# Patch embeddings of tiles 4 to 10 as three fp16 products instead of fp32, and one new wait on VectorE

## The reference, cut to what matters

```
out = jnp.einsum('bnp,dp->bnd', patches, W) + b            # patch embedding
h = jnp.concatenate([cls_tok broadcast, out], axis=1)      # 32 x 37 x 256
h = h + attn(layernorm(h), Wq, Wk, Wv, Wo, bo, betas, mem, z)
h = h + ffn(layernorm(h), shared_w1, shared_w2, experts_w1, experts_w2, gate_w)
```

## Time and profile before

| what | us |
|---|---|
| median of 3 runs | 326.65 (326.32 to 326.92) |
| profiled execution | 325.89 |
| its span in the trace | 324.0 |
| PE busy | 306.7 (95%) |
| DVE busy | 223.4 (69%) |
| ACT busy | 184.5 (57%) |
| POOL busy | 152.1 (47%) |

### The profile page before, as it was taken

The page is one execution under the profiler, slowest core; times in us unless marked ns, Lnnn a source line. Parts: engine busy times, 40 slices in busy tenths (PEclk is TensorE's granted clock), DMA queues, the critical chain, the costliest instruction groups (busy, mean ns, idle before and its releaser), DMA issues.

```text
span 324.0 us, 9888 instructions
## 1 busy us (share of the span) xinstructions
PE 306.7 (95%) x3521; PEld 259.6 (80%) x3521; DVE 223.4 (69%) x502; ACT 184.5 (57%) x355; POOL 152.1 (47%) x208
## 2 busy tenths in 40 slices
PE   8789999999998999999999999999999999999990
PEld 6678788988777999999997777777787787777870
DVE  0637888888898989999886868755554546565530
ACT  1366768878896978476768878733232332323220
POOL 0577747777586322112622344656353544434131
PEclk9999999999999999999999999999999999999998
DMA  7775335322241117814798774243323242333121
GB/s 231 260 222 210 108 111 179 111 83 77 77 124 58 32 31 205 269 24 95 195 275 309 185 239 110 45 67 41 60 42 59 34 67 35 54 48 46 22 34 16
DMA packets 18642, 36.37 MB, mean 112 GB/s; under 512 B 3331, under 2 KB 10982, under 8 KB 18598
## 3 DMA queue, kind: packets, MB, share of 16 engines
q1 hardware_dynamic: 12166, 27.71, 26.2%
q0 software_dynamic: 6432, 8.03, 16.3%
HBM read 28.52 MB, written 7.21 MB: 110 GB/s over the span
## 4 chain that ended last, share of the span: by engine, by line
PE 76%; DVE 9%; DMA 4%; POOL 3%; issue 3%; ACT 2%; SPq 1%; POOLq 1%; DVEq 0%; ACTq 0%
PE bank L820 21%; PE bank L833 14%; PE bank L643 7%; PE bank L835 6%; PE bank L500 6%; PE bank L602 6%; DMA out_rows<-y,add_id 2%; PE bank L525 2%; PE bank L551 2%; DMA weights<-in_patches 2%; PE bank L591 2%; PE bank L565 1%; PE bank L555 1%; DVE weights L1309 1%; PE bank L453 1%
## 5 line engine op out<-in xcount | busy, mean ns | idle before, releaser
L820 PEld LDWEIGHTS bank<-x_t,weights 128*128 x1248 | 87.5, 98 | 25.5 <-issue 0.2
L820 PE MATMUL bank<-x_t,weights 128*128 128x128 f16 x1248 | 103.8, 219 | 0.0
L1002 ACT ACTIVATE act_out<-bank 128x512 f32<-128x512 f32 (+2 forms) x72 | 42.0, 585 | 86.1 <-PE bank L820 71.8
L1270 POOL DMA_INDIRECT out_rows<-y,add_id x26 | 43.0, 1653 | 69.6 <-DVE y L1626 48.1
L833 PE MATMUL bank<-weights,hid_hi 128*128 x192 | 73.3, 382 | 0.2
L1417 DVE SCALAR_TENSOR_TENSOR hid_lo<-act_out,hid_hi 128x512 f16<-128x512 f32 (+2 forms) x72 | 48.6, 680 | 12.5 <-ACT hid_hi L1013 11.0
L835 PE MATMUL bank<-weights,hid_lo 128*128 x192 | 52.3, 273 | 0.0
L1423 DVE SCALAR_TENSOR_TENSOR weights<-stage,weights 128x1024 f16<-128x1024 f32 x36 | 43.0, 1221 | 0.7 <-ACT weights L959 0.7
L959 ACT ACTIVATE weights<-stage 128x1024 f16<-128x1024 f32 x36 | 36.8, 1049 | 0.0
L1237 POOL DMA_INDIRECT slot_rows<-x_rows,gather_id x26 | 28.0, 1075 | 13.0 <-DMA out_rows<-y 5.2
L500 PE MATMUL bank<-weights 128*111 128x256 f32 x132 | 31.3, 386 | 1.6 <-DMA weights<-in_patches 1.1
(11 more groups left out here) (164 smaller groups left out, 522.8 us busy)
## 6 DMA issues: line engine op xcount, KB each, us to landing
stage<-in_w_ffn SPq DMA_DIRECT2D x36, 512.0 KB
weights<-in_patches SPq DMA_DIRECT2D x11, 333.0 KB, 3.3
x_rows<-rows SPq DMA_DIRECT2D x11, 111.0 KB
out_rows<-weights SPq DMA_DIRECT2D x10, 111.0 KB
out_rows<-y POOLq DMA_DIRECT2D x9, 119.0 KB, 5.3
weights<-in_w_embed SPq DMA_DIRECT2D x3, 256.0 KB, 4.2
stage<-in_w_qk SPq DMA_DIRECT2D x1, 512.0 KB, 6.9
slot_rows<-x_rows,gather_id POOLq DMA_INDIRECT x26, 4.1
```

What stands on the lines that cost most here:

```text
L820: mm = nc.tensor.matmul(o, weights[:, bass.ds(base + 2 * k * CHUNK + 2 * (col - col % D) + w * D + col % D, P)], x_t[:, b, (2 * x + k) * P ...
L1002: nc.scalar.activation(d_, s_, ACT.Silu, scale=1.0 / (X_SCALE * W_SCALE)).then_inc(hid_acted, 1)
L1270: nc.gpsimd.indirect_dma_start(out=out, out_offset=bass.IndirectOffsetOnAxis(ap=add_id[:, j:j + 1], axis=0), in_=y[:, y_place(j)], in_offs ...
```

## The change

The weights of the embedding are split once into scaled fp16 high parts (ScalarE, ahead of its first other work) and low parts (VectorE, in step 1). From tile 4 on the patches of a tile are split too: ScalarE makes the high part at the end of step `t-4`, VectorE the low part in step `t-3` (those of tiles 4 and 5 at other places of steps 1 and 2). `embed(t)` is then 18 fp16 matmuls instead of 6 fp32 ones, and `embed_h` undoes the scale while it adds the bias. Tiles 0 to 3 stay fp32. The buffers of the pairs lie in memory that is used only later. The load of a patch buffer now waits for the low part of its last tenant from tile 4 on. From step 5 to step 10 VectorE waits for GpSimd's deviations of the step before, ahead of the weight chunk's low part, behind which the patches' low part now stands.

```diff
+F16_FROM = 4
+P_SCALE = 16.0
+EMBED_PRODUCTS = ((1, 0), (0, 1), (0, 0))
...
             def load_patches(t):
-                if t >= PATCH_RING:
-                    sp.wait_ge(embed_ready, t - PATCH_RING + 1)
+                held = t - PATCH_RING
+                if held >= F16_FROM:
+                    sp.wait_ge(patch_lo, held - F16_FROM + 1)
+                elif held >= 0:
+                    sp.wait_ge(embed_ready, held + 1)
...
             def embed(t):
-                pe.wait_ge(patches_in[t % PATCH_RING], 16 * (t // PATCH_RING + 1))
+                if t < F16_FROM:
+                    pe.wait_ge(patches_in[t % PATCH_RING], 16 * (t // PATCH_RING + 1))
+                else:
+                    pe.wait_ge(patch_lo, t - F16_FROM + 1)
+                if t == F16_FROM:
+                    pe.wait_ge(we_lo, 2)
...
+                if t >= F16_FROM:
+                    for n, (x, w) in enumerate(EMBED_PRODUCTS):
+                        for k in range(PC):
+                            we = we_front[:, k, w] if k < 4 else we_back[:, k - 4, w]
+                            mm = nc.tensor.matmul(embed_bank(t), patch_pair[t % 2][:, x, k * T:(k + 1) * T], we,
+                                                  start=(n == 0 and k == 0), stop=(n == 2 and k == PC - 1))
+                    mm.then_inc(embed_ready, 1)
+                    return
...
+            def split_patches_hi(t):
+                act.wait_ge(patches_in[t % PATCH_RING], 16 * (t // PATCH_RING + 1))
+                if t >= F16_FROM + 2:
+                    act.wait_ge(embed_ready, t - 1)
+                nc.scalar.mul(patch_pair[t % 2][:, 0], s_patch[:, t % PATCH_RING].rearrange("p a b -> p (a b)"),
+                              P_SCALE).then_inc(patch_hi, 1)
+
+            for part_ in range(EMBED_PARTS):
+                act.wait_ge(embed_in[part_], 16)
+                if part_ == 1:
+                    nc.scalar.mul(we_front[:, :, 0], s_we[:, 0:4], W_SCALE).then_inc(we_hi, 1)
+                if part_ == 2:
+                    nc.scalar.mul(we_back[:, :, 0], s_we[:, 4:], W_SCALE).then_inc(we_hi, 1)
...
+                if s in (1, 2):
+                    split_patches_hi(s + 3)
+                if 2 <= s < NT - 4:
+                    split_patches_hi(s + 4)
...
+            def split_patches_lo(t):
+                dve.wait_ge(patch_hi, t - F16_FROM + 1)
+                nc.vector.scalar_tensor_tensor(
+                    out=patch_pair[t % 2][:, 1], in0=s_patch[:, t % PATCH_RING].rearrange("p a b -> p (a b)"),
+                    scalar=P_SCALE, in1=patch_pair[t % 2][:, 0], op0=ALU.mult,
+                    op1=ALU.subtract).then_inc(patch_lo, 1)
...
+                if s == 1:
+                    we_lo_of(0, we_front, s_we[:, 0:4])
+                    we_lo_of(1, we_back, s_we[:, 4:])
...
+                if 5 <= s < NT:
+                    dve.wait_ge(rstd2, s - 4)
                 for c in chunks_at(s):
                     split_lo(c)
+                if 3 <= s < NT - 3:
+                    split_patches_lo(s + 3)
                 if s + 2 < NT:
                     embed_h(s + 2)
+                if s == 1:
+                    split_patches_lo(4)
...
+                    split_patches_lo(5)
```

More of the change, by code:

```diff
@@ L101, in build @@
         y = sb("y", [P, 3, D])
+        we_front = hid_hi.rearrange("p a b -> p (a b)").rearrange("p (k w d) -> p k w d", w=2, d=D)
+        we_back = hid_lo.rearrange("p a b -> p (a b)")[:, 0:2 * 2 * D].rearrange(
+            "p (k w d) -> p k w d", w=2, d=D)
+        patch_pair = [ap[:, 0:2 * PC * T].rearrange("p (w n) -> p w n", w=2) for ap in (
+            act_out.rearrange("p a b -> p (a b)").bitcast(F16),
+            slot_rows.rearrange("p a b -> p (a b)"))]
         space = weights[:, EARLY * EW:].bitcast(F32)
@@ L208, in build @@
         embed_ready = sem("embed_ready")
+        we_hi = sem("we_hi")
+        we_lo = sem("we_lo")
+        patch_hi = sem("patch_hi")
+        patch_lo = sem("patch_lo")
         h_ready = sem("h_ready")
@@ L1300, in embed_h @@
                     dve.wait_ge(rstd1, t - 1)
-                nc.vector.tensor_tensor(h[0:T, t % RING], embed_bank(t), s_eb[0:T],
-                                        ALU.add).then_inc(h_ready, 1)
+                if t < F16_FROM:
+                    nc.vector.tensor_tensor(h[0:T, t % RING], embed_bank(t), s_eb[0:T],
+                                            ALU.add).then_inc(h_ready, 1)
+                else:
+                    nc.vector.scalar_tensor_tensor(out=h[0:T, t % RING], in0=embed_bank(t),
+                                                   scalar=1.0 / (P_SCALE * W_SCALE), in1=s_eb[0:T],
+                                                   op0=ALU.mult, op1=ALU.add).then_inc(h_ready, 1)
                 dve.wait_ge(h_ready, t + 1)
@@ L1361, in proj_lo_of, with we_lo_of @@
                                                op0=ALU.mult, op1=ALU.subtract).then_inc(proj_lo, 1)
+            def we_lo_of(n, dst, src):
+                dve.wait_ge(we_hi, n + 1)
+                nc.vector.scalar_tensor_tensor(out=dst[:, :, 1], in0=src, scalar=W_SCALE, in1=dst[:, :, 0],
+                                               op0=ALU.mult, op1=ALU.subtract).then_inc(we_lo, 1)
+            def split_patches_lo(t):
[4 more added lines that the diff above has]
+                    op1=ALU.subtract).then_inc(patch_lo, 1)
             def xln_lo(t):
```

## The result

| | before | after |
|---|---|---|
| median of 5 runs, us | 326.65 (326.11 to 326.92) | 329.15 (328.54 to 329.70) |
| profiled execution / its span | 325.89 / 324.0 | 329.15 / 327.2 |
| end of step 4 | 45.93 | 46.56 |
| steps 5, 6, 7, 8 | 8.50, 8.96, 8.70, 8.87 | 9.80, 9.32, 9.46, 8.39 |
| end of step 8 | 80.96 | 83.53 |

The changed kernel is slower: ratio 1.0080, with an interval of 1.0067 to 1.0092. The forecast was 327.7; it had the sign, and less than half of the size (+1.05 against +2.5 on the medians). A step is counted as in the prediction, from the end of one `residual`'s statistics to the next. After step 10 the two kernels take the same time. The page's busy times: TensorE has 1.4 us less than before and VectorE 10 more.

The account below looks back on a forecast made before the run. It took TensorE as bound, with the GpSimd loop and VectorE close behind. Steps 1 to 4 +0.1, 5 to 7 +1.44, 8 -0.47: +1.07 on 325.89 gives 326.96, as median 327.7 us; own range 326.9 to 328.5, wide 323.8 to 329.6.

Parts of the forecast that it names:

- the wide range: Whole kernel: 323.8 to 329.6 us, leaving out TensorE's full gain and the sum of both slower rivals.
- the opened lock: Rival, steps 5 to 7: GpSimd's bias add runs between VectorE's two low parts; 9.7 us a step, 329.2 in all; chance 0.13.
- steps 5 to 7: Forecast at 9.2 us each, 27.6 against 26.16 before: +1.44 us.
- step 8: Shorter embedding and the wait, no patches' low part: `embed_h` at 4.75, end at 8.4 against 8.87, -0.47 us.
- The bias add waits behind both: Steps 5 to 7: GpSimd's bias add waits through both VectorE low parts, ends at 6.15, `row_lo` at 6.8 instead of 6.13.
- steps 1 to 4: VectorE's 5.1 us of added low parts against 5.6 us of idle time; end of step 4 moves by +0.1 us.
- the start is late: Rival, start: ScalarE's two extra high parts delay step 3's softmax; +1.5 in place of +0.1, 329.1 us; chance 0.11.
- The work and its order are the same: Behind step 8: nothing changes, so no time is added there.
- Hidden low parts: Rival, steps 5 to 7: patches' low part falls into VectorE's wait for the embedding; -1.0, 325.7 us; chance 0.30.

Follow-up runs that it names:

- fp32_embed: The changed kernel with all splits and waits, but tiles 4 to 10 embedded in fp32 as before; 328.96 us, ratio 1.0083 to the kernel before.
- no_wait: The changed kernel without VectorE's wait for GpSimd's deviations; 328.94 us, ratio 1.0112 to the kernel before.
- fill_clock: The changed kernel with 14 small fp16 matmuls behind `turn_xln` of step 5, where TensorE idled; 328.46 us, ratio 1.0079 to the kernel before.
- no_low: The changed kernel without the patches' low parts, the third product taking the high part again; 323.85 us, ratio 0.9934 to the kernel before.
- lo_on_gpsimd: The changed kernel with the low parts of tiles 7 to 10 made by GpSimd behind `relu_q`; 327.43 us, ratio 1.0050 to the kernel before.
- gpsimd_four: `lo_on_gpsimd` with `combine` rewritten so that no instruction has two operands in memory; 324.81 us, ratio 0.9953 to the kernel before.
- lo_no_port: The changed kernel with a one-input sum over the same 666 columns replacing each patches' low part; 326.74 us, ratio 1.0023 to the kernel before.
- lo_after_embed: The changed kernel with the patches' low part behind `embed_h` in steps 3 to 7; 326.77 us, ratio 1.0033 to the kernel before.
- lo_last_no_wait: The changed kernel without the wait, with the patches' low part behind `combine` in steps 3 to 7; 330.15 us, ratio 1.0106 to before.
- wait_only: The kernel before with only the new wait of VectorE for GpSimd's deviations; 325.47 us, ratio 0.9987 to the kernel before.

## Why the prediction was right and wrong

The measured 329.15 lies in the wide range and outside the forecast's own 326.9 to 328.5. It lies beside the opened lock, 329.2, to which 0.13 was given, and that the two totals agree so well is in part luck: that rival had 29.1 us for steps 5 to 7, which took 28.58, and +0.1 for the start and nothing for step 10, which together brought 1.22.

**Right.** The direction, and its reason: in steps 5 to 7 the shorter embedding is worth nothing as long as VectorE has the low part, `fp32_embed` against the changed kernel. The embedding takes 2.06 us (59.33 to 61.39 in step 6). The wait costs 0.54 us in step 5 (about 0.6 was forecast) and next to nothing later, and the last deviation is back at 0.25. At the release GpSimd's `xln_lo` comes first in steps 5 and 7 and the low part of the chunk is drawn out to 1.67 ("some 1.7"). TensorE waits for `row_lo`. `combine(0)` was forecast at 35.75 and was at 35.85. The start's splits of weights were hidden: ahead of `embed_h(3)` VectorE still waits for 1.37 us (3.10 before), and it begins 0.16 later, within the scatter of the start. The earlier trace rows were read too far, since the DMA share is 0.83 again in the microsecond after, but nothing hung on it: ScalarE's high part of tile 6 waited for no load.

**Right in size, step 8, and half in its reason.** It was forecast at 8.4 and is 8.39. The forecast worked it out from VectorE's queue, with `embed_h` 4.75 us into the step (measured 4.58), and no wait of VectorE is left there; so far it is right. But it gave the shorter embedding as what makes this possible, and `fp32_embed` has 8.40 with the long one. There TensorE, which had idled in steps 5 and 7, begins the embedding 1.65 us into the step (2.02 in step 7 of before) and is done in time. TensorE had time to spare there because the steps ahead were long, so the 0.48 us of step 8 are no measure of what the shorter embedding is worth.

**Wrong: steps 5 to 7.** The step that failed is "The bias add waits behind both". In steps 5 and 7 it ran between the two low parts, which is the rival to which 0.13 was given; only in step 6 did GpSimd wait through both. The mechanism that is shown in its place is GpSimd's turn between two instructions of VectorE. The rival has this order of events right, and its price was a little high: `embed_h` at 6.05 and 9.7 us were worked out, and in step 7 it started at 71.53, 5.85 into the step, which ended at 9.46. The forecast's 27.6 us for the three steps became 28.58, +0.98. Of it 0.16 is the clock's fall, net, for which the forecast had no term.

The reading of the earlier trace rows behind the failed step was right as a row and too narrow as evidence. There a GpSimd instruction stood still through two of VectorE's, and `no_wait` shows the same in its steps 6 and 7 (2.30 us in both)., priced as the less likely, show the other. The Trainium skill (SBUF — State Buffer, "Who interferes with whom") says that whoever issues first has the ports for the whole instruction; the traces agree with that where VectorE was held up (`xln_lo` starts 0.07 to 0.08 us ahead and the chunk's low part takes 1.67), they do not agree with it by the starts in step 6, and they show both outcomes between two in a row. What decides between them is open. In `no_wait` and in step 6 GpSimd's instruction has a start 0.12 to 0.22 us before VectorE's first, and lost to both. In steps 5 and 7 it started while VectorE's first, itself held up by `xln_lo`, was in progress, and got the next turn. In step 4 both show 40.29 and GpSimd's went first. In steps 5 to 7 of `fp32_embed` and `fill_clock` VectorE's first is held up each time (1.67 or 1.68) and GpSimd gets the next turn each time (1.37 for the second). The earlier trace rows don't fit that: there the first took its plain 1.22 and GpSimd got in all the same. These are the rows; the rule behind them was not found.

**Wrong: step 4.** The forecast gave steps 1 to 4 +0.1; they took +0.63, of which 0.16 was there at `embed_h(3)`. It costed a low part of the patches at its plain 0.85 and had no term for a meeting of the chunk's. But the bias add meets it there too:

```profile
39.66 0.67 POOL L1244 TENSOR_TENSOR x_t<-weights,x_t 111x256 f16<-111x256 f32 x1 [0.19 <-ACT x_t L1001]
...
40.29 0.72 POOL L1266 TENSOR_TENSOR weights<-weights 111x256 f32<-111x256 f32 x1
40.29 1.80 DVE L1488 SCALAR_TENSOR_TENSOR weights<-stage,weights 128x1024 f16<-128x1024 f32 x1
...
42.02 1.01 DVE L1423 SCALAR_TENSOR_TENSOR slot_rows<-weights,slot_rows 128x666 f16<-128x666 f32 x1
```

The chunk's takes 1.80, where it took 1.35 in step 4 of before, and the patches' 1.01 instead of 0.85. The first, 0.45 longer, and the shorter embedding use up the 0.81 us in which VectorE waited for the embedding there before, so the second has no cover left: from the start of `combine(0)` to the end of step 4 the changed kernel takes 10.71 us, and `no_low` and `lo_on_gpsimd`, whose chunk has the same 1.80 but behind which VectorE does no low part of patches in that step, take 9.93. In `gpsimd_four` the step ends at 45.82, 0.11 ahead of before, though VectorE still does the low part of tile 6 in step 3. The forecast's rival "the start is late" put its cost on ScalarE's queue; it was VectorE's low part without cover, drawn out by GpSimd, instead.

**Wrong: behind step 8.** "The work and its order are the same" holds for the instructions and not for the time. In the changed kernel's step 10 the two engines start 0.01 us apart, GpSimd has the ports, and `finish_sq` takes 0.98:

```profile
94.85 0.98 DVE L1366 SCALAR_TENSOR_TENSOR weights<-weights 128x222 f32<-128x222 f32 x1
94.86 0.72 POOL L1266 TENSOR_TENSOR weights<-weights 111x256 f32<-111x256 f32 x1
```

In the kernel before they start 0.03 apart and VectorE has them, 0.39:

```profile
92.28 0.39 DVE L1313 SCALAR_TENSOR_TENSOR weights<-weights 128x222 f32<-128x222 f32 x1
92.31 0.95 POOL L1218 TENSOR_TENSOR weights<-weights 111x256 f32<-111x256 f32 x1
```

That is 0.59 us of the 3.15 by which step 10 ended later. All fourteen kernels fall in two groups. In the changed one, `lo_no_port`, `lo_after_embed`, `fill_clock` and `lo_last_no_wait` GpSimd starts 0.01 us after VectorE, `finish_sq` takes 0.98 and the step 4.9 us. In the other nine GpSimd starts 0.02 to 0.11 after it, `finish_sq` takes 0.39 or 0.40 and the step 4.2 to 4.35. We see no edit that it follows. There is one profile of each kernel, so whether a kernel's other executions go the same way isn't known.

**The sum.** +0.63 for steps 1 to 4, +2.42 for 5 to 7, -0.48 for 8 and +0.59 for 10 make 3.16 us on the profiled executions (forecast: +0.1, +1.44, -0.47, 0). The medians differ by 2.5, since the profiled execution of before lay 0.76 under its median and that of after on it.

**The best rival.** "Hidden low parts", 0.30, fell with `no_low`: the low parts were never hidden, because the 0.7 us in which VectorE waits ahead of `embed_h` are the time in which TensorE's embedding is late, and the change takes just that away, by the shorter embedding and by the chunk's low part, which is longer by 0.46 once GpSimd goes first (with the wait alone, in `wait_only`, 0.43 and 0.19 us of it are left in steps 6 and 7). In step 6 of `no_low` `embed_h` starts at 58.36, as the chunk's low part ends (56.75 + 1.68), and waits for nothing. Making the embedding shorter and filling the wait for it are not two gains.

## What to carry to other kernels

When work moves from one engine to another, price it in the second engine's queue with the idle time that is left after the change, not the one in the trace. Where VectorE reads two operands in memory and GpSimd works beside it, each such instruction of this kernel could cost what was left of the other engine's, on either side; count how many meetings a step has, and take operands from PSUM or change the place until they don't meet. The added wait, which freed GpSimd's deviations from a block, moved the block to what was next in its queue. And when a forecast meets a number, as for step 8, look at the run that leaves the reason out.

## What the runs showed of the hardware

- Of two VectorE instructions back to back with two operands in memory, GpSimd is sometimes let in between (1.37 instead of 0.85 for the second) and sometimes not (its own at 2.68 and 2.30). When GpSimd's bias add started 0.01 us after VectorE's `finish_sq` (five kernels), VectorE was held up for 0.59 us; at 0.02 to 0.11 us after it (nine kernels), it was not.
- `scalar_tensor_tensor` takes part in this as `tensor_tensor` does (1.22 to 1.68, 0.39 to 1.54); a reduce with one input does not (0.81 to 0.85 in seven places of `lo_no_port`), nor does a form with one operand in PSUM (four in 0.86, beside GpSimd's 1.36).
- The granted clock fell to 0.50, its lower level, after 1.16 us of idle TensorE and was 0.62 in the microsecond from 56 and 1.00 from 57 on; four matmuls of 128x256 in fp32 took 1.94 instead of 1.07. 14 small matmuls in that gap (0.88 us in all) kept it at 1.00.
- A subtraction of 666 columns from fp32 to fp16 takes GpSimd 1.35 to 1.37 us (1.45 or 1.46 in some steps), and the low part of 666 columns takes VectorE 0.85.
